# Graph network layers on one core: the squares of three products written into their own accumulation bank instead of a scratch array

## The reference, cut to what matters

```
mu = out.mean(-1, keepdims=True)
var = ((out - mu) ** 2).mean(-1, keepdims=True)
return (out - mu) * jax.lax.rsqrt(var + LN_EPS) * g + beta
```

## Time and profile before

| what | value |
|---|---|
| runs | 2149.53 us median, 2148.34 to 2161.56 |
| the profiled execution's own time | 2153.21 us |
| its span, first to last instruction | 2151.5 us |
| ScalarE busy | 1543.9 us (72%) |
| VectorE busy | 1633.3 us (76%) |
| TensorE matmul busy | 1598.8 us (74%) |
| GpSimd busy | 1060.0 us (49%) |
| mean granted TensorE clock | 0.868 of full speed |

### The profile page before, as it was taken

How to read it: one execution, slowest core, us unless ns; L and a number is a source line. 1 busy time by engine, 2 the same in 40 slices (tenths; PEclk the granted TensorE clock), 3 DMA queues, 4 the chain that set the end, 5 groups by cost and what they waited for, 6 DMA issues and landing times. The chain is left out here.

```text
span 2151.5 us, 40995 instructions
## 1 busy us (share of the span) xinstructions
PE 1598.8 (74%) x9595; PEld 1206.1 (56%) x9595; DVE 1633.3 (76%) x8491; ACT 1543.9 (72%) x7842; POOL 1060.0 (49%) x919
## 2 busy tenths in 40 slices
PE   2589488888658886787597885796883996884960
PEld 1589355555347775454496552794542994542850
DVE  3581489999769996798686896786895786985960
ACT  0362199999659995798497995696993896992640
POOL 0477778600035553877003786005774007772877
PEclk9996599999879997799697997897996997995985
DMA  8013323311122112221323122223113123213421
GB/s 150 19 40 98 96 53 97 102 59 49 39 76 66 58 52 72 58 59 48 82 67 107 25 59 71 66 64 90 44 44 93 50 67 77 58 40 105 105 66 35
DMA packets 123136, 145.44 MB, mean 68 GB/s; under 512 B 56197, under 2 KB 83637, under 8 KB 122145
## 3 DMA queue, kind: packets, MB, share of 16 engines
q1 hardware_dynamic: 66303, 116.60, 19.5%
q0 software_dynamic: 56160, 25.44, 5.9%
q10 hardware_dynamic: 432, 0.79, 0.1%
HBM read 94.80 MB, written 68.06 MB: 76 GB/s over the span
## 5 line engine op out<-in xcount | busy, mean ns | idle before, releaser
L217 POOL DMA_INDIRECT S<-row_t,rowI x400 | 540.0, 1350 | 573.1 <-issue 573.1
L951 PE MATMUL bank<-AC,XT 128*125 128x390 f32 x800 | 326.3, 513 | 0.4
L1015 ACT ACTIVATE R<-bank 125x128 f32<-125x128 f32 x1200 | 320.8, 301 | 0.0
L1015 ACT ACTIVATION_READ_ACCUMULATOR R<-bank 125x1 f32 x1200 | 274.6, 236 | 0.0
L1741 PE MATMUL bank<-WCX,XT 128*125 128x130 f32 (+1 forms) x1400 | 218.4, 279 | 0.1
L205 PEld LDWEIGHTS bank<-ident,Y 125*128 125x128 f32 x800 | 97.9, 150 | 212.5 <-issue 137.6
L205 PE MATMUL bank<-ident,Y 125*128 125x125 f32 x800 | 131.1, 289 | 113.4 <-ACT XT L999 52.0
L1057 DVE BATCH_NORM_STATS2 st<-R 125x6 f32<-125x128 f32 x800 | 173.2, 279 | 33.2 <-issue 32.7
L217 POOL DMA_INDIRECT S<-in_x,srcI x100 | 131.3, 1313 | 111.9 <-issue 111.9
L1741 PEld LDWEIGHTS bank<-WCX,XT 128*125 128x125 f32 x1400 | 182.4, 188 | 6.8 <-ACT XT L1778 0.5
L931 PEld LDWEIGHTS bank<-AC,XT 128*125 128x125 f32 x800 | 104.6, 202 | 118.1 <-ACT SB L1032 111.6
(11 more groups left out here) (449 smaller groups left out, 4907.3 us busy)
## 6 DMA issues: line engine op xcount, KB each, us to landing
row_t<-T SPq DMA_DIRECT2D x40, 573.1 KB
R<-in_x SPq DMA_DIRECT2D x100, 224.0 KB
out_rows<-R SPq DMA_DIRECT2D x100, 224.0 KB
R<-m_t SPq DMA_DIRECT2D x5, 2734.4 KB
S<-row_t,rowI POOLq DMA_INDIRECT x400
T<-in_edge_attr SPq DMA_DIRECT2D x1, 5600.0 KB
x_t<-XB SPq DMA_DIRECT2D x50, 112.0 KB
R<-x_t SPq DMA_DIRECT2D x25, 224.0 KB
```

What stands on the lines that cost most here:

```text
L217: pool.indirect_dma_start(to, None, table, bass.IndirectOffsetOnAxis(ap=idx, axis=0), bounds_check=rows - 1, oob_is_err=False).then_inc(do ...
L951: nc.tensor.matmul(LAYERS[a][0:P, 0:3 * D + 6], h0(g, a), ACB[:, 0:3 * D + 6], start=True, stop=True).then_inc(layers_done.s, 1)
L1015: ins = nc.scalar.activation(JUNK[:, a * 3 + l, :], LAYERS[a][0:P, l * D:(l + 1) * D], ACT.Square, scale=D ** -0.5, accum_out=NRM[:, g % N ...
```

## The change

The squares of L1015 go to the columns that they were read from, in the accumulation bank, instead of to `JUNK`. The accumulated sums still go to `NRM`. The squares of the last product (L1037) still go to `JUNK`, now to its tiles 0 to 3. No instruction is added, taken away or moved on any engine, and every wait stays as it was.

```diff
@@ -1012,7 +1012,7 @@
                                 act.wait_ge(*third_sum.at(g - NS + 1))
                             nc.scalar.activation(DOT[:, g % NS, :, a], LAYERS[a][0:P, 3 * D:3 * D + 6], ACT.Copy)
                             for l in range(3):
-                                ins = nc.scalar.activation(JUNK[:, a * 3 + l, :], LAYERS[a][0:P, l * D:(l + 1) * D],
+                                ins = nc.scalar.activation(LAYERS[a][0:P, l * D:(l + 1) * D], LAYERS[a][0:P, l * D:(l + 1) * D],
                                                            ACT.Square, scale=D ** -0.5,
                                                            accum_out=NRM[:, g % NS, l, a:a + 1])
                             ins.then_inc(normed.s, 1)
@@ -1034,7 +1034,7 @@
                     def square_last(g):
                         act.wait_ge(*last_done.at(g + 1))
                         for a in range(Q):
-                            ins = nc.scalar.activation(JUNK[:, 12 + a, :], last_of(g)[:, a, :], ACT.Square,
+                            ins = nc.scalar.activation(JUNK[:, a, :], last_of(g)[:, a, :], ACT.Square,
                                                        scale=D ** -0.5, accum_out=ss4[:, g % NS, a:a + 1])
                         ins.then_inc(last_squared.s, 1)
```

## The result

| | before | after |
|---|---|---|
| median | 2149.37 us (7 runs) | 2172.48 us (7 runs, 2169.01 to 2174.22) |
| ratio | 1 | 1.0101, 95% interval 1.0087 to 1.0116 |
| profiled execution, its span | 2153.21, 2151.5 us | 2173.21, 2171.5 us |

A forecast was written before the change was run, and what follows sets the result against it. The prediction took ScalarE and VectorE as both full in the steady dense stages. Four terms of 0 added to the profiled 2153.21 us gave 2153, or 2149 us for the median, range 2138 to 2163.

The forecast's parts named there:

- What bounds the kernel: Steady dense stages: ScalarE (571.78 of 572.00 us) and VectorE (569.51) both full; TensorE at 497.79 has room.
- The step of the square: L1015, start to next start: the destination does not enter its 0.16 us; 0 change, bounds -0.05 to +0.107 us.
- one line: ScalarE's copies L999 and L1013 and the square: 0.83 ns per element plus some 0.05 us, no destination term.
- its own signs: Slow signs: square 0.19 us or more, or read grown; group period over 8.8 us; VectorE waiting on ScalarE in steady stretch.
- The accumulator read: Read behind each square, into NRM: stays 0.09 us, 0 change, bounds -0.03 to +0.12 us.
- The room on ScalarE: Wait hidden in L986's step: 0.08 us per group, in which about 7 ns per square would vanish.
- The slow rival: L1015: bank read and written in turn, +0.107 us per square, +102 us, 2252 us; chance 0.05 for the full price.
- A partial price above 28 ns: Part of the slow rival at L1015, costing more than 21.5 us in all; chance 0.07.
- The cap on a gain: Steady stretches: VectorE leaves only 2.5 us; beyond about 3 us per stage the gathers would hold the end.
- The range: Whole kernel: 2138 to 2163 us, holding a gain down to 11 us and a slow loss up to 13.
- the slow cases: L1015 longer: chance 0.12 for a loss above 1% (21.5 us), 0.04 for one below it.

## Why the prediction was wrong, point by point

- **What bounds the kernel**: held in the main. ScalarE and VectorE are both full in the dense stages, durations are not steps, and the losses lie where they were looked for. That VectorE sets 8.52 us is supported twice: freeing ScalarE of about 0.4 us a group moved nothing in the steady groups, and VectorE's own distance is 8.53 us even where ScalarE still runs at 8.1 to 8.4.
- **The step of the square**: this is the step that failed. It was put at 0 because two copies and a square from a bank fit one line; it is +0.040 us, with 1200 of them. All three rows of that line write to SBUF, and so does whatever stands ahead of them: the fit could not hold a term for the destination, let alone for a change of it. "The fixed part goes by where the operand is read" is true of the rows and says nothing of the case without a row. The value lay inside the bounds that I had set (-0.05 to +0.107) and I took their inner point. Of its own signs, the step of 0.19 or more came (0.197), VectorE's waits on ScalarE only grew from 0.4 to 2.7 us in 250, and the period stayed just under the 8.8 that was named (8.77).
- **The accumulator read**: put at 0, measured -0.005. Near enough, and its tie to its *own* destination (0.05 us into a bank) was not seen.
- **The room on ScalarE**: put at 0.08 us a group from L986 alone, measured 0.42 - 0.24 = 0.18, since the steps of L993 and L1032 hold waits too. It exists only in the steady groups: the first full ones of a stage have periods of 8.3 to 8.4 us, ScalarE's own steps and no more.
- **The slow rival**: right in sign and place, wrong in mechanism and in its full price (0.107 us). A partial price above 28 ns was given 0.07. With the measured 0.035 us and 0.18 us of room, 100 groups give 100 x (12 x 0.035 - 0.18) = 24 us, against 23.7 in the dense stages and 23.1 in the medians. That agreement is partly luck: the trace has 18.6 of the 23.7 us in the middle of the stages and 5.6 at their ends, for which the formula has no term.
- **The cap on a gain**: held. With 0.4 us a group less on ScalarE the kernel gained 0.2%, not the 2% that 100 x 0.4 us would be.
- **The range**: both unknown costs were bounded, but 2163 as its upper end takes in only 13 of the 102 us that lay between the bounds. With one operation without any row and an engine without room behind it, the share of the slow cases should have been larger. Losses of 13 to 21 us, which were counted in the slow rival's 0.04, lay outside the range too.
- The Trainium skill, "ScalarE: Activation LUTs", section "Step-by-step: what each stage is for", calls PSUM the lower-latency port. The runs agree as to latency, and only where the destination stays: behind another bank write a square's record can be as short as 0.21 us, and into SBUF none was under 0.25. As to what a square costs its engine the measurement decides: the step is the same 0.157 us, and 0.04 us longer behind a write to SBUF.

## What to carry to other kernels

On an engine with no room, price an instruction by the distance between starts, and treat a pair of source and destination that no row shows as a cost with a sign you don't know, not as zero. A write's price can depend on the instruction ahead of it: keep ScalarE's bank writes together and send their small results to a bank too, instead of alternating with SBUF. A stage that fills and drains pays for a longer step in its last groups as well, where a saving or a loss per period says nothing. Before moving a wait of TensorE, look whether its granted clock survives it.

## What the runs showed of the hardware that I had not expected

- ScalarE, source in a bank, 122 or 128 columns: a write to a bank right behind a write to SBUF holds the engine 0.04 us longer (0.19 against 0.15); behind another bank write it doesn't, and a write to SBUF behind one to a bank doesn't either. With the source in SBUF (61 or 122 columns), or with 32 columns, nothing of it is seen; with 64 the square has its 0.04 and the read behind it gives it back.
- An accumulator read takes 0.09 us into SBUF and 0.05 into a bank; behind a square of 64 columns in a bank it takes 0.05 into SBUF too.
- Moving one copy by one place in ScalarE's list, with no work added, let TensorE's clock fall in the steady stretch and cost 2.3%.
